# The routed experts' loop on TensorE, written out block by block, with its register loads moved

## The chip, the cores and the metric

The kernel runs on one core of one Trainium2 chip. The metric is the device time of one execution in microseconds (us). Three executions of the kernel before took 1186.09, 1189.49 and 1204.87 us; their median, 1189.49 us, is the time that the prediction is made against.

## The reference, cut to what matters

One transformer layer over x of shape (2, 2048, 512): a cross-attention by correlation against a context of 128 rows, and then a feed-forward part with a shared expert of 1024 hidden columns and 16 routed experts of 128 hidden columns. The change lies in the routed experts alone:

```python
topk_idx, w, _scores = _route(xf, router_w, correction_bias)   # 4 experts of 16 for each of 4096 rows
g = jnp.einsum('sc,ech->esh', xf, gate_w)                      # 512 -> 128
u = jnp.einsum('sc,ech->esh', xf, up_w)                        # 512 -> 128
h = jax.nn.silu(g) * u
hw = h * combine.T[:, :, None]                                 # the weights of the chosen four, else 0
routed = jnp.einsum('esh,ehc->sc', hw, down_w)                 # 128 -> 512
```

The kernel does not compute all 16 experts for all rows. It sorts the 4096 x 4 pairs of row and expert into blocks of 128 rows of one expert, and computes each block once.

## The kernel before, in words

Five programs, one for each engine, run side by side and meet in semaphores. The routed stage comes after attention, the shared expert of most rows and the routing. It handles `BLOCKS` = 144 blocks of 128 rows. Which expert a block belongs to is known only on the chip: VectorE writes a table `blocks_e`, and TensorE loads eight entries of it at a time into registers (`experts`, line 875) and uses them as addresses of the expert's weights, which lie in SBUF as high and low fp16 halves.

What happens to block s:

- GpSimd gathers its 128 rows from `xr_dram` into one of four buffers `xg` (an indirect DMA, line 1599, behind a small copy of indices, line 1587). Block s uses buffer s mod 4. For an odd block the buffer is free when the DMA that turned the rows of block s-4 has landed; for an even one, when TensorE has turned them. GpSimd issues the gathers strictly in order.
- The rows are turned so that the 512 input columns lie on partitions. Even blocks are turned by TensorE (`turn_rows`, 8 transposes, line 885) and copied out by VectorE (line 1463). Odd blocks are turned by a DMA transpose that SyncE issues (`turn_odd`, lines 538 and 539) into one of two buffers `xgT_odd`.
- `gate_up` (line 900): 12 matmuls, the gate and up columns together. ScalarE takes the silu (line 1116), VectorE multiplies (line 1477), ScalarE and VectorE split the product into high and low fp16 (lines 1120 and 1480).
- `turn_h` (line 911): two transposes of the product, copied out by VectorE (line 1469). `down` (line 919): three matmuls. ScalarE copies the result to SBUF (`save_y`, line 1126), one of two buffers, and SyncE writes it to `y_dram` (`y_out`, line 530).

TensorE's program is software-pipelined: in the step of block s it does `gate_up` of s+1, `turn_h` of s and `down` of s-1, with `turn_rows` of a later even block ahead of every second step. Four such steps are one pass of `four(i)`. The first pass is written out with constant counts; a loop (`pe.Fori`, line 940) makes the other 34 passes; the last steps are written out again. Inside the loop a semaphore count that depends on s is worked out in a register before the wait (lines 881, 892, 894, and parts of 883, 896 and 917), and each pass begins with `experts(4 * i)`, the register load of line 875.

SyncE's program is in order too. For each four blocks it issues: the turn of one odd block, two results out, the turn of the other odd block, two results out. A turn waits for its gather and for the `gate_up` that last read its buffer; a result waits for ScalarE's copy.

The other four engines keep their loops over the blocks.

Of the kernel before, what the change touches and what calls it, by code (L numbers as in the profile page):

```python
# [52 lines left out]
BLOCKS = (NP + E * (P - 1)) // P + 1  # L53
# [63 lines left out]
def build(nc, x, ctxT, wk, wqT, wv, wo, biases, bo, cb, routerT, gu_w, dn_w, const, const_r, out):  # L117
    with ExitStack() as ctx:
# [145 lines left out]
        def only(v, i, *rest):  # L264

            v = v[(slice(None), bass.ds(i, 1)) + rest]
            names = "abcd"[:len(v.shape) - 1]
            if len(v.shape) == 3:
                return v.rearrange("p a b -> p (a b)")
            return v.rearrange("p a b c -> p (a b) c")  # L270
# [330 lines left out]
        def _(pe):  # L601
# [181 lines left out]
            with pe.Fori(1, NB // 2) as i:  # L783

                a, b, s = 2 * i, 2 * i + 1, i - 1
# [87 lines left out]
            def experts(at):  # L873

                return nc.values_load_multi_w_load_instructions(
                    blocks_e[0:1, bass.ds(at, 8)], engines=[mybir.EngineType.PE], min_val=0, max_val=E - 1,
                    skip_runtime_bounds_check_because="VectorE counts at most E - 1 experts before a block")[1]

            def turn_rows(u, j, fresh):

                pe.wait_ge(s_xg[2 * j], 16 * ((u >> 1) + 1))
                if not fresh:
                    pe.wait_ge(s_txe, u - 1)
                for n in range(2 * KC):
                    last = turn(bank16[j][:, n * P:n * P + P], xg[:, 2 * j, n * P:n * P + P], id16)  # L885
                last.then_inc(s_tx, 1)

            def gate_up(s, r, e, fresh):

                j, rows = r % 2, (xgT, xgT_odd)[r % 2]  # L890
                if r % 2:
                    pe.wait_ge(s_odd[r // 2], 16 * ((s >> 2) + 1))
                else:
                    pe.wait_ge(s_txe, (s >> 1) + 1)
                if not fresh:
                    pe.wait_ge(s_rh, s - 1)
                n = 0
                for xv, wp in PARTS:
                    for kc in range(KC):
                        last = mm(bank[2 + j][:, 0:2 * H], rows[:, r // 2, xv * KC + kc, :],  # L900
                                  only((gu_hi_r, gu_lo_r)[wp], e, slice(kc * 2 * H, (kc + 1) * 2 * H)),
                                  start=(n == 0), stop=(n == 3 * KC - 1))
                        n += 1
                last.then_inc(s_rg, 1)

            def turn_h(s, j, fresh):
                pe.wait_ge(s_rhl, s + 1)
                if not fresh:
                    pe.wait_ge(s_hte, s - 1)
                for v in range(2):  # L910
                    last = turn(bank16[4 + j][:, v * P:v * P + P], r_hb[:, j, v, :], id16)
                last.then_inc(s_ht, 1)

            def down(s, j, e, fresh):
                pe.wait_ge(s_hte, s + 1)
                if not fresh:
                    pe.wait_ge(s_ye, s - 1)
                for n, (hv, wp) in enumerate(PARTS):
                    last = mm(bank[6 + j][:, :], r_hT[:, j, hv, :], only((dn_hi_r, dn_lo_r)[wp], e),  # L919
                              start=(n == 0), stop=(n == 2))  # L920
                last.then_inc(s_rd, 1)

            e = experts(0)
            turn_rows(0, 0, True)
            gate_up(0, 0, e[0], True)
            turn_rows(1, 1, True)
            gate_up(1, 1, e[1], True)
            turn_h(0, 0, True)
            def four(i, first):
                e = experts(4 * i)  # L930
                for n in range(4):
                    s = 4 * i + 1 + n
                    if n % 2:
                        turn_rows(2 * i + 2 + n // 2, n // 2, False)
                    gate_up(s + 1, (n + 2) % 4, e[n + 2], False)
                    turn_h(s, (1 + n) % 2, first and n == 0)
                    down(s - 1, n % 2, e[n], first and n < 2)

            four(0, True)
            with pe.Fori(1, BLOCKS // 4 - 1) as i:  # L940
                four(i, False)
            e = experts(BLOCKS - 4)
            gate_up(BLOCKS - 2, 2, e[2], False)
            turn_h(BLOCKS - 3, 1, False)
            down(BLOCKS - 4, 0, e[0], False)
            gate_up(BLOCKS - 1, 3, e[3], False)
            turn_h(BLOCKS - 2, 0, False)
            down(BLOCKS - 3, 1, e[1], False)
            turn_h(BLOCKS - 1, 1, False)
            down(BLOCKS - 2, 0, e[2], False)  # L950
            down(BLOCKS - 1, 1, e[3], False)


            pe.wait_ge(s_ye, BLOCKS)
# [733 lines left out]
```

## Time and profile before

| what | value |
|---|---|
| three executions | 1186.09, 1189.49, 1204.87 us |
| profiled execution: its span | 1205.0 us |
| profiled execution: its own time | not marked among the three; the longest, 1204.87 us, lies 0.13 us under the span |
| TensorE busy | 1046.4 us (87%) |
| VectorE, ScalarE, GpSimd busy | 638.2, 386.1, 444.0 us |
| DMA over the span | 191 GB/s on average |
| passes of the loop | from 571.4 to 944.4 us of the span |

Busy time is the union of an engine's instructions. TensorE's matmuls overlap, so its busy time counts a pipeline that is not empty, not one that is full. Instructions that an engine's sequencer handles alone (register operations, waits, branches, register loads, DMA issues) are not counted as busy; the profile marks them with a q behind the engine's name. "Issue" as a releaser means that the engine sat idle while nothing that the profile shows held it. The granted clock of TensorE is given as a share of 2.4 GHz.

### The profile page before, as it was taken

What the parts mean: (1) busy time and instruction counts of PE and PEld (TensorE: products, weight loads), DVE (VectorE), ACT (ScalarE), POOL (GpSimd) and SP (SyncE); (2) the same over time, 40 slices, a digit from 0 to 9 for tenths busy, and PEclk for the clock granted to TensorE, in tenths of its full rate; (3) what the DMA queues carried; (4) which work ended last, traced back from release to release, by engine and by line L of the source; (5) the groups of instructions that cost most, each with busy time, mean ns of one, the idle gap of its engine ahead of it and who ended that gap; (6) DMA issues with size and microseconds to landing.
All of it is one profiled execution on the core that took longest, in us unless ns stands there. A gap on an engine that the chain in (4) does not pass through costs nothing.

```text
span 1205.0 us, 22651 instructions
## 1 busy us (share of the span) xinstructions
PE 1046.4 (87%) x6496; PEld 603.5 (50%) x6497; DVE 638.2 (53%) x1454; ACT 386.1 (32%) x751; POOL 444.0 (37%) x517
## 2 busy tenths in 40 slices
PE   7899499899999988886789999889899877878597
PEld 6576344444444433434566676666666533323243
DVE  4935567533434877995333444434344246547455
ACT  2423243232323544441334443434344301111011
POOL 1730320111100424225334444344444286846650
PEclk9988789999999999997999999999999998989899
DMA  9605763563329315215999999989899686897750
GB/s 348 238 19 179 191 227 106 160 181 113 139 79 222 136 53 184 78 53 128 269 262 244 255 259 260 233 236 227 235 245 255 208 260 198 200 239 238 252 176 35
DMA packets 219262, 229.57 MB, mean 191 GB/s; under 512 B 143670, under 2 KB 152664, under 8 KB 218712
## 3 DMA queue, kind: packets, MB, share of 16 engines
q1 hardware_dynamic: 195676, 151.53, 44.1%
q0 software_dynamic: 23552, 77.61, 22.9%
q8 instruction: 17, 0.28, 0.1%
q14 instruction: 17, 0.14, 0.0%
HBM read 124.99 MB, written 70.55 MB: 162 GB/s over the span
## 4 chain that ended last, share of the span: by engine, by line
PE 44%; DVE 16%; issue 14%; DMA 13%; ACT 4%; another core or an unknown queue 4%; POOL 2%; SPq 1%; DVEq 1%; ACTq 0%; POOLq 0%
PE bank L750 13%; PE bank L900 11%; DMA arena<-arena 6%; PE bank L766 5%; PE bank L919 5%; DVE arena L1516 3%; DMA arena<-xr_dram,arena 2%; PE bank L731 2%; PE bank L885 2%; DVE arena L1274 2%; DVE arena L1450 1%; DMA y_dram<-arena 1%; DMA arena<-xr_dram 1%; PE bank L607 1%
## 5 line engine op out<-in xcount | busy, mean ns | idle before, releaser
L750 PE MATMUL bank<-arena 128*128 (+1 forms) x1536 | 361.3, 394 | 53.9 <-DVE arena L1274 27.3
L750 PEld LDWEIGHTS bank<-arena 128*128 128x128 f16 (+1 forms) x1536 | 154.1, 101 | 252.1 <-issue 65.2
L900 PE MATMUL bank<-arena 128*128 x1728 | 224.5, 278 | 34.0 <-issue 18.6
L900 PEld LDWEIGHTS bank<-arena 128*128 128x128 f16 x1728 | 162.8, 98 | 90.2 <-issue 55.9
L766 PE MATMUL bank<-arena 128*128 128x512 f16 (+1 forms) x768 | 176.2, 380 | 5.5 <-DVE arena L1276 5.5
L1599 POOL DMA_INDIRECT arena<-xr_dram,arena x144 | 141.2, 980 | 55.9 <-issue 43.9
L1629 POOL DMA_INDIRECT arena<-y_dram,arena x128 | 135.2, 1056 | 38.7 <-issue 34.2
L1477 DVE SCALAR_TENSOR_TENSOR arena<-bank,arena 128x128 f32<-128x128 f32 x144 | 41.9, 291 | 178.6 <-ACT arena L1116 140.4
L1053 ACT ACTIVATE arena<-arena 128x512 f16<-128x512 f32 x64 | 40.3, 630 | 262.1 <-DVE arena L1274 235.9
L766 PEld LDWEIGHTS bank<-arena 128*128 128x128 f16 x768 | 74.9, 98 | 96.9 <-DVE arena L1276 6.6
L919 PE MATMUL bank<-arena 128*128 x432 | 117.1, 380 | 0.7
L1274 DVE SCALAR_TENSOR_TENSOR arena<-bank,arena 128x512 f32<-128x512 f32 x64 | 44.0, 688 | 138.3 <-PE bank L750 82.0
L1516 DVE SCALAR_TENSOR_TENSOR arena<-arena 128x512 f32<-128x512 f32 x128 | 96.7, 759 | 29.7 <-DMA arena<-y_dram,arena 10.8
L1546 POOL TENSOR_TENSOR arena<-arena 128x2048 f16<-128x2048 f32 x8 | 32.5, 4066 | 200.8 <-ACT arena L1029 200.8
L1126 ACT ACTIVATE arena<-bank 128x512 f32<-128x512 f32 x144 | 84.5, 587 | 55.2 <-DMA y_dram<-arena 44.9
L1046 ACT ACTIVATE arena<-bank 128x512 f32<-128x512 f32 x64 | 38.0, 594 | 171.4 <-PE bank L750 132.3
L1587 POOL COPY arena<-arena 128x1 int32 (+1 forms) x144 | 26.8, 186 | 165.8 <-DMA arena<-arena 115.9
L1116 ACT ACTIVATE arena<-bank 128x128 f32<-128x128 f32 x144 | 39.8, 276 | 136.7 <-PE bank L900 103.5
L1572 POOL TENSOR_TENSOR arena<-arena 128x1024 f32 x16 | 34.2, 2137 | 128.2 <-ACT arena L1102 128.2
L1480 DVE TENSOR_TENSOR arena<-arena 128x128 f16<-128x128 f32 x144 | 42.2, 293 | 54.0 <-ACT arena L1120 45.4
L1276 DVE TENSOR_TENSOR arena<-arena 128x512 f16<-128x512 f32 x64 | 45.0, 702 | 46.2 <-ACT arena L1053 41.9
L1120 ACT ACTIVATE arena<-arena 128x128 f16<-128x128 f32 x144 | 44.5, 309 | 58.7 <-DVE arena L1477 47.4
(173 smaller groups left out, 1130.5 us busy)
## 6 DMA issues: line engine op xcount, KB each, us to landing
y_dram<-arena SPq DMA_DIRECT2D x144, 256.0 KB
arena<-in_x SPq DMA_DIRECT2D x8, 1024.0 KB, 12.4
xr_dram<-arena SPq DMA_DIRECT2D x16, 512.0 KB, 2.9
x_dram<-arena SPq DMA_DIRECT2D x8, 1024.0 KB, 4.7
arena<-x_dram SPq DMA_DIRECT2D x8, 1024.0 KB
arena<-in_gu_w SPq DMA_DIRECT2D x16, 512.0 KB, 3.2
x1s_dram<-arena SPq DMA_DIRECT2D x5, 1024.0 KB, 6.5
arena<-x1s_dram SPq DMA_DIRECT2D x20, 256.0 KB
```

The costliest lines, as they stand in the source:

```text
L750: last = mm(bank[g][:, :], w, xt(xv * KC + kc), start=(n == 0), stop=(n == 3 * KC - 1))
L766: last = mm(bank[2 + t][:, :], s_hb[:, half, hv, t * P:t * P + P], only((dn_hi_s, dn_lo_s)[wp], c), start=(first and n == 0), stop=(final ...
L900: last = mm(bank[2 + j][:, 0:2 * H], rows[:, r // 2, xv * KC + kc, :], only((gu_hi_r, gu_lo_r)[wp], e, slice(kc * 2 * H, (kc + 1) * 2 * H) ...
L919: last = mm(bank[6 + j][:, :], r_hT[:, j, hv, :], only((dn_hi_r, dn_lo_r)[wp], e), start=(n == 0), stop=(n == 2))
L1120: A(r_hb[:, j, 0, :], r_h[:, j, :], ACT.Copy).then_inc(s_rhh, 1)
L1126: A(y_sb[:, j, :], bank[6 + j][:, :], ACT.Copy, scale=1.0 / WS).then_inc(s_ye, 1)
L1274: V.scalar_tensor_tensor(s_h, bank[1][:, :], 1.0 / WS, s_silu, ALU.mult, ALU.mult).then_inc(s_sh32, 1)
L1276: V.tensor_tensor(s_hb[:, h, 1, :], s_h, s_hb[:, h, 0, :], ALU.subtract).then_inc(s_shl, 1)
L1480: V.tensor_tensor(r_hb[:, j, 1, :], r_h[:, j, :], r_hb[:, j, 0, :], ALU.subtract).then_inc(s_rhl, 1)
L1516: V.scalar_tensor_tensor(acc, ybuf[p % RING][:, e, :], w, acc, ALU.mult, ALU.add).then_inc(s_cmb, 1)
L1599: pool.indirect_dma_start(out=xg[:, r % 4, :], out_offset=None, in_=xr_dram[:, :], in_offset=bass.IndirectOffsetOnAxis(ap=token_now[:, r:r ...
L1629: pool.indirect_dma_start(out=ybuf[p % RING][:, e, :], out_offset=None, in_=y_dram[:, :], in_offset=bass.IndirectOffsetOnAxis(ap=row_now[: ...
```

## The change

TensorE's program of the routed stage no longer has a loop. All steps from block 1 to block 143 are written out with the same order of work inside a step, and every semaphore count is a constant. The registers of the next four blocks are loaded in the third step of each group of four (`ahead`), ahead of that step's `gate_up`, and are taken over (`here = ahead`) at the group's end; before, they were loaded at the head of the group that uses them. No matmul, no transfer and no other engine's program is changed.

```diff
-            e = experts(0)
+            here, ahead = experts(0), None
             turn_rows(0, 0, True)
-            gate_up(0, 0, e[0], True)
+            gate_up(0, 0, here[0], True)
             turn_rows(1, 1, True)
-            gate_up(1, 1, e[1], True)
+            gate_up(1, 1, here[1], True)
             turn_h(0, 0, True)
-            def four(i, first):
-                e = experts(4 * i)
-                for n in range(4):
-                    s = 4 * i + 1 + n
-                    if n % 2:
-                        turn_rows(2 * i + 2 + n // 2, n // 2, False)
-                    gate_up(s + 1, (n + 2) % 4, e[n + 2], False)
-                    turn_h(s, (1 + n) % 2, first and n == 0)
-                    down(s - 1, n % 2, e[n], first and n < 2)
-
-            four(0, True)
-            with pe.Fori(1, BLOCKS // 4 - 1) as i:
-                four(i, False)
-            e = experts(BLOCKS - 4)
-            gate_up(BLOCKS - 2, 2, e[2], False)
...
+            for s in range(1, BLOCKS):
+
+                n = (s - 1) % 4
+                if n == 2 and s + 2 < BLOCKS:
+                    ahead = experts(s + 1)
+                if n % 2 and (s + 3) // 2 < BLOCKS // 2:
+                    turn_rows((s + 3) // 2, n // 2, False)
+                if s + 1 < BLOCKS:
+                    gate_up(s + 1, (n + 2) % 4, here[n + 2], False)
+                turn_h(s, s % 2, s == 1)
+                down(s - 1, n % 2, here[n], s <= 2)
+                if n == 3:
+                    here = ahead
+            down(BLOCKS - 1, 1, here[3], False)
```

## Rows read from the trace of the kernel before

**Rows 1.** The page's first line: the span.

```profile
span 1205.0 us, 22651 instructions
```

**Rows 2.** Windows: length, busy (count) of PE, PEld, DVE, ACT, POOL, clock, DMA, GB/s.

```profile
613.60:746.60 133.00, 124.99 (x1091) 91.80 (x1089) 56.47 (x182) 57.13 (x156) 60.85 (x106) 1.00 0.97 255
746.60:944.40 197.80, 179.45 (x1517) 129.64 (x1515) 78.36 (x252) 79.97 (x217) 81.14 (x138) 0.98 0.92 237
571.40:613.60 42.20, 30.95 (x261) 21.86 (x260) 13.09 (x43) 13.85 (x37) 13.93 (x24) 1.00 1.04 266
```

**Rows 3.** Chain of waits, 613.6 to 746.6 us: shares of the stretch by line.

```profile
by line: PE bank L900 52.4%; PE bank L919 24.5%; PE bank L885 8.4%; issue 5.5%; PE bank L911 4.4%; another core or an unknown queue 2.4%; DVE arena L1477 0.7%; ACT arena L1116 0.6%; ACT arena L1120 0.6%; DVE arena L1480 0.5%; ACT arena L112
```

**Rows 4.** Chain of waits, 860 to 945 us, its pieces: start, length, what.

```profile
869.16 3.65 DMA arena<-xr_dram,arena
...
879.78 3.69 DMA arena<-xr_dram,arena
...
889.95 4.50 DMA arena<-xr_dram,arena
```

**Rows 5.** Timeline of TensorE's matmuls: start, length, line, count, idle time before.

```profile
810.33 1.47 PE L900 MATMUL bank<-arena 128*128 x12
...
812.85 1.47 PE L900 MATMUL bank<-arena 128*128 x12
...
815.83 1.63 PE L900 MATMUL bank<-arena 128*128 x12 [0.75 <-issue]
...
818.50 1.47 PE L900 MATMUL bank<-arena 128*128 x12
...
820.57 1.47 PE L900 MATMUL bank<-arena 128*128 x12
```

**Rows 6.** Waits of TensorE, 571.4 to 944.4 us: total us, times, longest.

```profile
PE bank L900 <- issue: 18.4, 28, 1.4
PE bank L900 <- DMA arena<-arena: 13.3, 13, 3.2
```

**Rows 7.** TensorE's sequencer by line: ns least/median/most, first and last start in us.

```profile
L875 PEldq TENSOR_LOAD <-arena x37: 588/703/1245, 553.0 to 944.4; - x37
L940 PEldq COMPARE_BRANCH  x34: 76/208/228, 584.6 to 944.3; - x34
L881 PEldq FUSED_REGOPS  x68: 82/88/96, 574.3 to 941.1; - x68
L894 PEldq FUSED_REGOPS  x68: 68/69/69, 572.4 to 938.8; - x68
```

**Rows 8.** Timeline of GpSimd: gathers of every second odd block.

```profile
612.47 0.98 POOL L1599 DMA_INDIRECT arena<-xr_dram,arena  x1 [0.50 <-POOL arena L1587]
...
622.39 0.98 POOL L1599 DMA_INDIRECT arena<-xr_dram,arena  x1 [0.50 <-PE bank L885]
...
632.66 0.98 POOL L1599 DMA_INDIRECT arena<-xr_dram,arena  x1 [0.50 <-POOL arena L1587]
```

**Rows 9.** Timeline of SyncE's issues: the turn of the first of these blocks.

```profile
616.36 1.51 SPq L539 DMA_TRANSPOSE arena<-arena  x1
```

**Rows 10.** Waits of SyncE's queue, 571 to 950 us: total us, times, longest.

```profile
SPq L530 <- ACT arena L1126: 113.0, 72, 4.4
SPq L538 <- DMA arena<-xr_dram,arena: 20.9, 22, 3.1
```

**Rows 11.** Waits of GpSimd, 571 to 950 us.

```profile
POOL arena L1587 <- DMA arena<-arena: 112.0, 48, 5.9
POOL arena L1587 <- PE bank L885: 41.2, 27, 4.5
```

**Rows 12.** DMA queues, 569.5 to 571 us: packets, MB, share of 16 engines.

```profile
q8 instruction: 1, 0.02, 4.0%
```

**Rows 13.** The same for 556 to 584 us.

```profile
q8 instruction: 2, 0.03, 0.4%
```

**Rows 14.** Timeline of TensorE's matmuls: the group that runs across the packet of rows 12.

```profile
570.44 1.47 PE L900 MATMUL bank<-arena 128*128 x12
```

More of the change, by code:

```diff
@@ L921, in down @@
                 last.then_inc(s_rd, 1)
-            e = experts(0)
+            here, ahead = experts(0), None
             turn_rows(0, 0, True)
-            gate_up(0, 0, e[0], True)
+            gate_up(0, 0, here[0], True)
             turn_rows(1, 1, True)
-            gate_up(1, 1, e[1], True)
+            gate_up(1, 1, here[1], True)
             turn_h(0, 0, True)
-            def four(i, first):
-                e = experts(4 * i)
-                for n in range(4):
-                    s = 4 * i + 1 + n
-                    if n % 2:
-                        turn_rows(2 * i + 2 + n // 2, n // 2, False)
-                    gate_up(s + 1, (n + 2) % 4, e[n + 2], False)
-                    turn_h(s, (1 + n) % 2, first and n == 0)
-                    down(s - 1, n % 2, e[n], first and n < 2)
-            four(0, True)
-            with pe.Fori(1, BLOCKS // 4 - 1) as i:
-                four(i, False)
-            e = experts(BLOCKS - 4)
-            gate_up(BLOCKS - 2, 2, e[2], False)
[L944 to L951, printed above, removed]
+            for s in range(1, BLOCKS):
[11 more added lines that the diff above has]
+            down(BLOCKS - 1, 1, here[3], False)
             pe.wait_ge(s_ye, BLOCKS)
```

## The prediction, made before the changed kernel ran

> **What bounds the kernel now.** I read the span first [rows 1], then the loop in windows. A pass of four blocks is 84 matmuls (48 of gate_up, 12 of down, 8 of turn_h, 16 of turn_rows), so the counts of [rows 2] say how many passes each stretch holds: 13 in 133.0 us (10.23 us a pass), 18 in 197.8 us (10.99), and 3 in the first 42.2 us (14.07). Three stretches, three regimes.
>
> In the middle stretch the chain of waits is TensorE's own: its four lines hold 52.4 + 24.5 + 8.4 + 4.4 = 89.7% [rows 3]. In the last stretch the chain often leaves TensorE: it goes from a gather through a DMA turn to the next gather into the same buffer, and the gathers in it start 10.62 and then 10.17 us apart [rows 4]. The first stretch is slow for TensorE's waiting on turned rows: of the loop's 13.3 us of such waits [rows 6], the longest is 3.2 us, and its DMA share is 1.04 [rows 2].
>
> Next the timeline of matmuls over one pass [rows 5]. A step without turn_rows starts 2.07 us after the one before it (818.50 to 820.57), one with turn_rows 2.52 us (810.33 to 812.85). Two of each are 9.18 us. At the loop's back edge the step takes 2.98 us instead of 2.07 (812.85 to 815.83, 0.75 us of it idle by "issue"), and the step after it 2.67 instead of 2.52, because the first group of twelve matmuls runs for 1.63 us instead of 1.47: it is fed as it is issued. Together 0.91 + 0.15 = 1.06 us, and 9.18 + 1.06 = 10.24 us is the middle stretch's pass of 10.23. So there TensorE is the bound, and the back edge is all it loses. Over 34 passes the idle time alone is 18.4 us [rows 6]; with what hides in matmul spacing it is at most 34 x 1.06 = 36 us.
>
> **The change part by part.** *Branch and loop counter.* 34 branches of 0.208 us [rows 7] leave the sequencer at the place where TensorE runs dry. *Counts.* Two register operations at line 881 of 0.088 us, two alike at line 892 and two at line 894 of 0.069 us leave each pass [rows 7], 0.49 us of sequencer time; the waits themselves stay. *Register load.* It is not removed: one for each four blocks, 0.588 to 1.245 us, median 0.703 [rows 7]. It moves from behind the branch to the head of the third step. As it is in the sequencer's order, what hides it is the work already handed to TensorE, and not the two blocks until its values are used. At the third step at least turn_h and down are queued behind gate_up: 2.07 - 1.47 = 0.60 us by [rows 5]. At the back edge the same queue left 18.4 / 34 = 0.54 us idle on average. Without the branch (0.21) and the head's threshold (0.07) that is 0.26 us; I take 0.25 us for the moved load, spacing included. Its bounds are nothing (hidden, as it should be with more lead) and 0.91 us (the gap just moves to the third step). The 0.49 us of sequencer work that goes speaks for the low end, the long loads for the high one. So TensorE's own pass becomes 10.24 - (1.06 - 0.25) = 9.43 us, between 9.18 and 10.09: alone worth 0.81 x 34 = 27 us, at most 36.
>
> The rows show the gap at the back edge 28 times [rows 6]. The Trainium skill, Advanced Engine Details and Errata, section Engine Queue Depths, gives TensorE a queue of 64 entries. By that, 32 matmuls with their weight loads would lie ahead, some 3.5 us by an estimate from the pass, and neither branch nor load could be felt: nothing to win, 1189 us. The trace does not agree: 0.75 us was idle behind them.
>
> *Code.* Straight code is fetched. Two packets came in the 28 us in which the written-out first pass ran [rows 13]; one packet held 4.0% of 16 engines over 1.5 us, that is one engine for 0.96 us [rows 12]. About one for each four steps is new, some 34. TensorE's group of twelve started and ran across that packet without an idle mark [rows 14]; I take nothing for TensorE, and nothing for the transfers, with 0.96 us a pass as the upper bound. DMA engines and other queues see no other new work.
>
> *What is late next.* The odd blocks' rows. The gather for block s+4 waits for the turn of block s, the turn of s+4 for that gather. Two rounds of this loop in the middle stretch took 9.92 and 10.27 us [rows 8], with 3.89 us from gather to turn and 6.03 us from turn to the next gather in the first of them [rows 8, 9]. GpSimd waited 112.0 us for turns, against 41.2 us for TensorE [rows 11]. So a second loop, without TensorE in it, runs at nearly TensorE's present pace, and 9.43 us is below all four rounds shown. It is not wholly free of TensorE: SyncE waited 113.0 us in 72 cases for results ahead of its turns and only 20.9 us in 22 for the gather itself [rows 10]; a faster TensorE takes some of that away.
>
> *The sum.* Middle stretch: a pass of 9.92 us, the shorter round, instead of 10.23: 0.31 x 13 = 4.0 us. Bounds: 0 (10.27 holds) and 0.81 x 13. Last stretch: 0.2 x 18 = 3.6 us, between 0 (the chain of [rows 4]) and 0.81 x 18; I take near the low end because four tenths of its 10.99 us and more are above both loops and are not the back edge. First stretch: 0, it waits for data. Together 8 us; the end after the loop moves with it. The profiled span of 1205.0 becomes 1197 us. It is 15.5 us longer than the median of the runs, 1189.5, which the change should move by as much: **1181.5 us**.
>
> **The rivals.** *A. TensorE's gain passes through.* For it: the chain of [rows 3], and SyncE's 113.0 us, which make turns late for TensorE's sake, so that the row loop would shrink along. Against: [rows 8] and [rows 4], rounds without TensorE that take 9.92 to 10.62 us. 27 us: 1162 us; with no cost of the load left, 1153 us.
>
> *B. Nothing moves.* The load stops the sequencer as long in the third step (the 0.91 us end), or the row loop holds 10.2 us everywhere; the change then doesn't do what its text says. For it: the load is still in order, and the gather rounds average 10.25 us over [rows 4, 8], equal to the pass. Against: the branch and counts do go. 1189 us.
>
> *C. Slower: fetched code on the row loop.* Each pass brings a packet that holds one DMA engine for 0.96 us [rows 12]; a turn or gather has landed only when its last engine is done, so a packet in the wrong place lengthens a round by as much. In every pass: 34 x 0.96 = 33 us, less the 8: 1214 us. It decides the sign from 0.24 us a pass, which eats the 8 us, and 2% from 0.94 us. For it: a DMA share of 0.92 to 1.04 [rows 2]. Against: [rows 14], and that half the rounds have slack by [rows 10]. The Trainium skill, DMA: Bandwidth & Descriptors, section Queues, rings and completion order, has each engine alternate between queues and finish a whole packet first. By that rule such a packet does delay its engine's other work; no run here yet shows by how much a turn was late for it.
>
> **How the numbers follow.** Forecast 0.57, A 0.20, B 0.15, C 0.08. The range takes in A's 1162 and B's 1189, with room for the spread of the runs seen: 1160 to 1194 us. Outside lie C, A's extreme and noise, under 2 in 10. Around 2% is what a measurement of this kernel can tell from no change: below 1165.7 us or above 1213.3 us. Faster by that: most of A, 0.14, and 0.02 of the forecast's tail, so 0.16. Slower: most of C, 0.06. Within: 0.78.
>
> **What would show it.** No branch on TensorE; its waits by "issue" at gate_up down from 18.4 us to under 9; waits for turned rows (13.3 us) and for gathers on SyncE (20.9 us) up, since the bound moves there; passes of 9.9 to 10.1 us in a calm stretch. Passes of 9.4 us with TensorE's lines in the chain mean A. The same "issue" time, in the third step, means B. About 34 packets on q8 must appear; idle time on TensorE just behind them, or turns that land later by about 1 us, mean C. The forecast is wrong if the row loop's round falls well below 9.9 us.

## The result, and the profile after

The changed kernel took 1217.37 us (median of 4 executions, 1209.3 to 1221.29), the kernel before on the same occasion 1190.07 us (4 executions): ratio **1.019 [1.014, 1.024]**. It is slower; the prediction was 1181.5 us, in a range that ended at 1194. Run again later beside other kernels, it took 1225.91 us against 1209.21 us, 1.012 [1.004, 1.019]. The medians here take in every execution, and each ratio, with its interval, only those in the faster of the two states in which executions come, so that it is not the quotient of the medians.

A measure for these ratios: the kernel before, measured twice against itself, came out at 1.009 [1.003, 1.016] and at 0.995 [0.989, 1.001]. So the intervals are too narrow by about a hundredth, and a difference of about one per cent or less is called none. The loss itself is 16.7 to 27.3 us by the medians.

The page of the changed kernel, its span and its DMA queues (packets, MB, share of 16 engines), stands against [rows 1]:

```profile
span 1214.8 us, 22342 instructions
...
q1 hardware_dynamic: 195676, 151.53, 47.0%
q0 software_dynamic: 23552, 77.61, 22.7%
q8 instruction: 45, 0.74, 0.3%
```

q1 carries the turns of odd blocks and the results, q0 the gathers, q8 fetched code. Before, q8 had 17 packets and q1 needed 44.1% of a span of 1205.0 us for the same 195,676 packets. That is 16 x (0.470 x 1214.8 - 0.441 x 1205.0) = 633 us more of engine time for the same bytes; q0 has no more than before (22.9%).

The windows of the changed kernel, with the columns of [rows 2]:

```profile
571.40:613.60 42.20, 32.08 (x249) 22.72 (x248) 12.77 (x41) 13.12 (x36) 12.86 (x22) 0.84 1.03 231
613.60:746.60 133.00, 119.78 (x1000) 85.64 (x998) 51.86 (x167) 51.91 (x143) 56.35 (x96) 0.97 1.00 239
746.60:944.40 197.80, 174.61 (x1465) 125.25 (x1464) 75.73 (x243) 78.00 (x210) 82.11 (x140) 0.98 1.01 233
```

At 84 matmuls a pass the middle stretch now takes 11.2 us a pass (10.23 before), the last one 11.3 (10.99). In these two stretches the DMA share rose while GB/s fell. The chain of waits of the middle stretch answers to [rows 3], where TensorE's four lines held 89.7%:

```profile
by line: DMA arena<-arena 40.8%; PE bank L900 24.5%; DMA arena<-xr_dram,arena 11.4%; PE bank L919 10.8%; issue 5.0%; PE bank L885 3.0%; PE bank L911 2.0%; another core or an unknown queue 1.5%; ACT arena L1117 1.4%; DVE arena L1468 1.1%; AC
```

Turns and gathers hold 52.2%, TensorE 40.3%. The two profiles compared here lie further apart than the kernels do. The chain of the same stretch in the third profile of the kernel before, and in the second of the changed kernel:

```profile
by line: PE bank L900 34.1%; DMA arena<-arena 29.6%; PE bank L919 14.6%; DMA arena<-xr_dram,arena 9.6%; issue 5.2%; PE bank L885 4.7%; PE bank L911 2.8%; ACT arena L1126 1.3%; DVE arena L1477 1.1%; ACT arena L1116 1.1%; SPq L530 0.9%; ACT a
```

```profile
by line: PE bank L900 22.7%; DMA arena<-arena 18.4%; DMA y_dram<-arena 10.9%; PE bank L919 10.7%; issue 9.7%; DMA arena<-xr_dram,arena 8.1%; PE bank L885 3.0%; SPq L539 3.0%; ACT arena L1117 2.3%; SPq L530 2.0%; PE bank L911 1.9%; another c
```

TensorE holds 56.2% in the one (78.4% in the kernel's second profile) and 38.3% in the other. By the counts of matmuls a pass of this stretch takes 10.8 us in the second and third profiles of the kernel before, and 11.2 us in both of the changed kernel; the last stretch takes 10.7 to 11.0 us in the former and 10.9 and 11.3 in the latter.

TensorE's waits (571.4 to 944.4 us), SyncE's and GpSimd's (571 to 950 us), and its register load (least/median/most ns) follow; they answer to [rows 6, 10, 11, 7].

```profile
PE bank L900 <- DMA arena<-arena: 30.4, 20, 7.6
...
PE bank L900 <- issue: 2.2, 8, 0.6
```

```profile
SPq L538 <- DMA arena<-xr_dram,arena: 28.0, 28, 3.2
```

```profile
POOL arena L1578 <- DMA arena<-arena: 150.3, 54, 9.9
...
POOL arena L1578 <- PE bank L885: 21.9, 18, 3.0
```

```profile
L875 PEldq TENSOR_LOAD <-arena x36: 587/690/1914, 553.1 to 961.5; - x36
```

The gap by "issue" did go, from 18.4 to 2.2 us (14.7 and 14.8 in the other profiles of the kernel before, 4.7 in the second of the changed one), and GpSimd waits for turns 38.3 us longer (112.0 to 150.3; the other profiles have 118.4 and 126.2 before, 139.1 after). TensorE waits for turned rows instead in this pair of profiles (13.3 to 30.4 us), but that does not separate the kernels: it is 19.8 and 22.6 us in the other two before, and 19.4 in the second after.

**The row loop, measured.** A round of an odd block is: gather from issue to its last packet, time until SyncE issues the turn, turn from issue to its last packet, time until the next gather into the same buffer is issued. The table gives means in us over the 46 to 56 rounds, from the seventh four blocks on, whose packets can be told apart (64 of 4,096 bytes a gather, 1,024 of 256 bytes a turn), and the mean time of one turn packet over the routed stage. Its kernels are those of the experiments below.

| kernel | gather | to the turn | turn | to the next | round | turn packet, ns |
|---|---|---|---|---|---|---|
| before | 4.03 | 1.43 | 3.58 | 1.67 | 10.71 | 25.0 |
| before, second profile | 3.95 | 1.28 | 3.76 | 1.69 | 10.67 | 26.1 |
| before, third profile | 4.00 | 1.10 | 3.85 | 1.73 | 10.69 | 27.7 |
| changed | 4.25 | 0.97 | 4.17 | 1.76 | 11.14 | 33.4 |
| changed, second profile | 4.10 | 1.14 | 4.16 | 1.62 | 11.01 | 30.4 |
| written | 4.25 | 0.93 | 4.01 | 1.78 | 10.97 | 32.3 |
| inject4 | 4.24 | 1.18 | 4.14 | 1.97 | 11.53 | 33.1 |
| deep | 3.94 | 2.76 | 3.75 | -0.10 | 10.35 | 21.9 |
| deep4 | 4.03 | 2.64 | 3.84 | -0.25 | 10.26 | 23.5 |
| deep_after | 4.76 | 2.95 | 4.21 | -1.36 | 10.56 | 30.9 |

From before to changed (means over their profiles) the turn takes 0.44 us more and the gather 0.18, and the time to the turn shrinks by 0.22: 0.39 us a round, 13 us over 34 passes, of a loss of 17 to 27 us. In the profiled executions that is about all of it: their spans average 1205.3 us before and 1215.9 changed, and the gate_up of block 24 begins 78.1, 85.6 and 86.4 us after the first gather before, 85.8 and 80.7 us changed, so the loss lies behind it. Where the rest of the 17 to 27 us goes, no trace shows. A round is as long as a pass whatever holds the pass, so its length alone does not say that this loop is the bound; `deep`, below, tests that.

### The profile page after: what moved, and what is told of

It reads as the page before. It is cut to its first block, busy times and chain, and to the rows that moved or that the text cites. A ratio compares the mean times of both kernels' runs of the same rounds, so it can differ in the third digit from the quotient of the medians.

```text
span 1214.8 us, 22342 instructions
## 1 busy us (share of the span) xinstructions
PE 1055.9 (87%) x6496; PEld 606.7 (50%) x6496; DVE 638.8 (53%) x1454; ACT 387.0 (32%) x751; POOL 447.9 (37%) x517
## 3 DMA queue, kind: packets, MB, share of 16 engines
q1 hardware_dynamic: 195676, 151.53, 47.0%
## 4 chain that ended last, share of the span: by engine, by line
PE 36%; DMA 21%; DVE 15%; issue 13%; another core or an unknown queue 5%; ACT 4%; POOL 3%; SPq 1%; DVEq 1%; POOLq 0%; ACTq 0%
PE bank L750 14%; DMA arena<-arena 11%; DMA arena<-xr_dram,arena 6%; PE bank L766 6%; PE bank L900 5%; PE bank L919 2%; DMA y_dram<-arena 2%; POOL arena L1620 2%; DVE arena L1507 2%; PE bank L731 2%; DVE arena L1441 1%; DVE arena L1265 1%; PE bank L607 1%; PE bank L627 1%
## 5 line engine op out<-in xcount | busy, mean ns | idle before, releaser
L750 PE MATMUL bank<-arena 128*128 (+1 forms) x1536 | 356.8, 390 | 38.3 <-ACT arena L1037 14.2
L900 PE MATMUL bank<-arena 128*128 x1728 | 228.7, 282 | 39.1 <-DMA arena<-arena 32.9
L900 PEld LDWEIGHTS bank<-arena 128*128 128x128 f16 x1728 | 165.9, 100 | 96.8 <-issue 60.7
L766 PE MATMUL bank<-arena 128*128 128x512 f16 (+1 forms) x768 | 179.0, 382 | 10.7 <-DVE arena L1267 8.8
L766 PEld LDWEIGHTS bank<-arena 128*128 128x128 f16 x768 | 75.1, 99 | 103.7 <-DVE arena L1267 10.5
L919 PE MATMUL bank<-arena 128*128 x432 | 120.5, 389 | 0.6 <-DVE arena L1460 0.3
L1265 DVE SCALAR_TENSOR_TENSOR arena<-bank,arena 128x512 f32<-128x512 f32 x64 | 44.1, 689 | 133.5 <-PE bank L750 76.4
```

Source lines behind the costliest of these rows:

```text
L750: last = mm(bank[g][:, :], w, xt(xv * KC + kc), start=(n == 0), stop=(n == 3 * KC - 1))
L766: last = mm(bank[2 + t][:, :], s_hb[:, half, hv, t * P:t * P + P], only((dn_hi_s, dn_lo_s)[wp], c), start=(first and n == 0), stop=(final ...
L1265: V.scalar_tensor_tensor(s_h, bank[1][:, :], 1.0 / WS, s_silu, ALU.mult, ALU.mult).then_inc(s_sh32, 1)
```

## The experiments

**Pace or fetched code.** The change does two things at once: it feeds TensorE better, and it makes it fetch code all the time. `paced` takes the first back: eight useless matmuls of 256 columns, some 0.87 us, ahead of the first gate_up of each four blocks of the changed kernel.

```diff
+                for _ in range(extra):
+                    mm(bank[2 + j][:, 0:2 * H], rows[:, r // 2, 0, :], gu_hi_r[:, 0, 0:2 * H], start=True, stop=True)
```

> The changed kernel, written out, with eight matmuls of no use ahead of the first gate_up of each four blocks (0.109 us each, 0.87 us a pass, overwritten by the true ones), so that TensorE's own pass is as long as before, about 10.2 us, while the code is fetched as in the changed kernel and a little more. Theory F: 1210 to 1230 us, turn packets at 33 ns or more. Theory P: back to 1190 us, turn packets near 25 ns.

1221.45 against 1202.41 us, 1.013 [1.003, 1.023]; 48 packets on q8, 32.7 ns a turn packet. With TensorE held up by 0.88 us a pass (808.75 to 809.63 us in its trace) turn packets are still longer on average, and the ratio lies above one still, if little above what the kernel before showed against itself.

`written` is the other half: the kernel before with its loop written out, the register load left at the head of each four blocks.

```diff
-            with pe.Fori(1, BLOCKS // 4 - 1) as i:
+            for i in range(1, BLOCKS // 4 - 1):
                 four(i, False)
```

> The loop of before written out and nothing else: the register load stays at the head of each four blocks, without lead. Theory F (the instruction packets stretch the DMA turns, and the row loop with them): some 30 packets on q8 in the routed stage, a turn's packet of 256 bytes from 25 ns to 31-34 ns, ratio 1.010 to 1.020. Theory P (the loss comes from a TensorE that runs ahead, the fetch costs nothing): TensorE's gap at each four blocks is still there, so the ratio is 0.995 to 1.005.

1219.26 against 1208.47 us, 1.014 [0.999, 1.028]; on time alone that is no clear difference. The trace is clear. DMA queues from 613.6 to 930 us, first of the kernel before, then of written, then of the changed kernel:

```profile
q1 hardware_dynamic: 78544, 46.22, 57.1%
```

```profile
q1 hardware_dynamic: 77397, 45.21, 63.7%
...
q8 instruction: 25, 0.41, 0.6%
```

```profile
q1 hardware_dynamic: 76368, 44.74, 65.1%
...
q8 instruction: 25, 0.41, 0.6%
```

Twenty-five packets of code, 0.6% of the engines' time, go with 6.6 to 8.0 points more for q1, which moves less than before in that stretch. With the other profiles (58.2 and 60.2% before, 61.6% changed) the step is smaller and has the same sign. Per MB, q1's share is 1.24 points in the kernel before (57.1 / 46.22; 1.25 and 1.29 in its other profiles), 1.41 in written and 1.46 in the changed kernel. Of all kernels here, those without steady fetching lie at 1.13 to 1.31 and those with it at 1.35 to 1.46; inject4, below, lies at 1.42. The waits of TensorE in written, 571 to 950 us:

```profile
PE bank L900 <- DMA arena<-arena: 32.6, 21, 7.9
...
PE bank L900 <- issue: 3.5, 11, 0.8
```

The gap by "issue" is nearly gone here too, without any lead for the load.

**Which turns are longer.** Not all of them, and not all packets: the median turn packet takes 18 ns in both kernels, and the mean rises by a few long ones. Of the 61,440 packets of the 60 turns from the seventh four blocks on, 49, 73 and 97 took over 1 us in the profiles of the kernel before, 436 and 335 in those of the changed kernel, and 380 in written. In the changed kernel some nine in ten of these begin within 3 us of the start of a packet of code. The turns can be parted by whether a packet of code was on an engine while they ran:

| kernel | turns with code | us | packets over 1 us in each | turns without | us | packets over 1 us in each |
|---|---|---|---|---|---|---|
| before, three profiles | 0 | | | 60 | 3.64 to 3.81 | 0.8 to 1.6 |
| changed | 27 | 4.60 | 14.5 | 33 | 3.93 | 1.3 |
| changed, second profile | 22 | 4.67 | 13.1 | 38 | 3.72 | 1.2 |
| paced | 30 | 4.70 | 8.8 | 30 | 3.22 | 0.5 |
| written | 24 | 4.09 | 12.2 | 36 | 3.93 | 2.4 |

A turn that meets a packet of code has about ten times the long packets and takes 0.67 and 0.95 us more in the changed kernel (0.16 in written, whose other turns hold some more long packets too); the others are much as before. A longer turn meets a packet more easily, but chance moments laid on the turns of the kernel before pick turns at most 0.2 us longer than its mean. Packets of results (2,048 bytes) and of gathers (4,096) did not get longer on average: 88.9 and 245.8 ns before, 87.5 and 241.7 changed (613.6 to 930 us).

**TensorE's pace without fetching.** Here the loop stays, with 1, 4, 8 or 17 passes a body, and the load moves to the head of the third step:

```diff
+            def group(p, final=False):
+                e = experts(4 * p + 2)
+                for m in range(4):
+                    n, s = (m + 2) % 4, 4 * p + 3 + m
...
+            with pe.Fori(0, 8) as i:
+                for w in range(4):
+                    group(4 * i + 2 + w)
```

> One part of the change alone: the loop of one pass a body stays, with its 34 branches and counts in registers; only the register load stands ahead of the third step and not of the first. No code is fetched in the loop. Theory F and theory P both expect about the kernel before, 1185 to 1195 us, since branch and load still stand together; under P it could lose a little if TensorE gets faster by it.

> TensorE keeps a loop, but of 8 iterations of four passes each (16 blocks a body); two passes and the ends are written out, and the registers are loaded ahead of the third step, as in the changed kernel. So TensorE is nearly as fast as in the changed kernel (26 of 34 branches gone), while its code should be fetched once and then stay. Theory F (the 16 KB packets of fetched code hold up the DMA turns of the odd blocks): few packets on q8 in the loop, turn packets back near 25 ns on average, total at or under the kernel before, 1175 to 1190 us. Theory P (a faster TensorE alone makes turns, gathers and result writes collide; the fetches are innocent): turn packets stay near 33 ns and the total stays at 1205 to 1220 us.

> The same program as the loop of four passes a body, but with 17 passes a body and 2 iterations: a body too long to stay, as far as one can guess, so that about 28 packets of code come over q8 in the routed stage, at the same pace of TensorE. Theory F: 1205 to 1220 us, like the changed kernel. Theory P: the same time as the loop of four passes a body. If few packets come on q8, it says nothing against F and should be as fast as the short body.

All three were far slower, and for a reason that had nothing to do with the question: 1.090 [1.081, 1.100], 1.080 [1.070, 1.090] and 1.083 [1.074, 1.093]. Register load and waits of TensorE (571 to 1040 us) in loop1:

```profile
L875 PEldq TENSOR_LOAD <-arena x37: 777/2573/5071, 551.2 to 1041.5; - x37
```

```profile
PE bank L900 <- issue: 93.7, 34, 4.8
```

The load's median went from 703 ns [rows 7] to 2,573. It now starts at entry 4p + 2 of the table, 8 bytes off a multiple of 16. The next kernels move the table by two entries, so that the same load starts at such a multiple:

```diff
-        blocks_e = little(BLOCKS + 8, I32)
+        blocks_e = little(BLOCKS + 12, I32)[:, 2:BLOCKS + 10]
```

> The loop of four passes a body again, with the table of experts moved by two entries, so that each register load starts at a multiple of four entries (16 bytes) as in the kernels before and after; in the first trial the load started two entries off and took 2.8 us. If the start is what made it slow, loads are back at 0.6 to 1.2 us and the total falls by about 100 us. Theory F (fetched code holds up the turns): few packets on q8 in the loop, turn packets near 25 ns, total 1165 to 1190 us on a chip where the kernel before takes 1190, so a ratio of 0.98 to 1.00. Theory P (a faster TensorE alone makes the transfers collide): ratio 1.01 to 1.02, turn packets at 33 ns.

> The same program with 8 passes a body and 4 iterations. If the code of eight passes stays, it is as fast as the loop of four passes or 1 to 3 us faster, with few packets on q8; if it is fetched anew in each iteration, theory F puts it with the loop of 17 passes and theory P with the loop of four.

> The same program with 17 passes a body, and the table moved likewise. The first trial showed 48 packets on q8, 30 of them in the routed stage, as many as in the changed kernel. Theory F: slower than the loop of four passes by 1.5 to 3%, ratio to the kernel before 1.01 to 1.02, turn packets at 30 ns or more. Theory P: the same as the loop of four passes.

> The loop of before with one pass of four blocks a body, the load moved to the head of the third step and its address at a multiple of 16 bytes; nothing is written out but the first and last blocks. Theory F: no fetch in the loop, turn packets at 25 ns, the load's lead no longer needed by anything: ratio 0.995 to 1.005. Theory P: ratio 1.005 to 1.015, as with four passes a body. If the load still takes 2.8 us the misaligned address was not the cause, and the ratio is near 1.09.

even4 took 1213.87 us, 1.010 [1.005, 1.015]; even1 1210.1 us, 1.011 [1.005, 1.017]; both are called none, if barely: on its own occasion even1 stands beside a kernel before that came out at 1.009. even8 took 1230.6 us, 1.026 [1.022, 1.030]; even17 1225.27 us, 1.017 [1.012, 1.023]. The median load is 0.73 to 0.88 us again in all four. The queues of even4 and of even8, 613.6 to 930 us:

```profile
q1 hardware_dynamic: 78769, 46.09, 60.4%
...
q8 instruction: 3, 0.05, 0.1%
```

```profile
q8 instruction: 30, 0.49, 0.7%
```

A body of four passes is fetched once and then runs without fetching; a body of eight is fetched again in each round. The two kernels with the fetching are the slower ones: turns that meet a packet of code take 4.25 us in even8 and 4.44 in even17, the others 3.66 and 3.58. But their time does not show what that costs, because a second cost came with it: TensorE itself waits for code where the loop jumps back. The branch and TensorE's waits by "issue" (571 to 950 us) in even8, then the branch in even4:

```profile
L951 PEldq COMPARE_BRANCH  x4: 79/4958/5689, 698.4 to 978.8; - x4
```

```profile
PE bank L900 <- issue: 26.1, 16, 6.5
```

```profile
L951 PEldq COMPARE_BRANCH  x8: 76/208/231, 645.0 to 950.5; - x8
```

The three jumps back of even8 leave TensorE idle for 6.4, 6.5 and 4.8 us, 17.6 us in all, about as much as the 16.7 us by which it is slower than even4; the one of even17 leaves 4.4 of 11.4 us. The written-out kernels have no jump and no such wait. The two loops without steady fetching did not win either: waits by "issue" were 8.0 us in even4 and 21.2 in even1, and neither number shows in the time. So by time alone kernels with and without fetching are hardly parted (paced 1.013, written 1.014; even4 1.010, even1 1.011); it is the turns that part them.

**Packets of that size by themselves.** ScalarE issues copies of 16,372 bytes from DRAM to DRAM, outside the computation, in the kernel before: one a pass (inject) or one a block (inject4).

```diff
+                for n in range(4):
+                    act.dma_start(spare_dram[bass.ds(4 * i + n, 1)], gu_flat).then_inc(s_spare, 16)
```

> The kernel before, and for each pass of its loops ScalarE issues one copy of 16372 bytes in HBM whose result nothing reads (35 of them), sized so that it should not be cut over the DMA engines. This puts the suspected traffic alone into the kernel before. Theory F: turn packets above 28 ns, and the total up by 8 to 30 us (ratio 1.007 to 1.025), if the copy goes as one long packet on one engine; if the trace shows it in short packets over many engines it tells less. Theory P: ratio 1.00, turn packets at 25 ns.

> The kernel before with one copy of 16,372 bytes from DRAM to DRAM for each block, four a pass, issued by ScalarE; the copies are not part of the computation. Theory F: four times the disturbance of one copy a pass (1.004, 27.3 ns): turn packets 31 to 36 ns, ratio 1.012 to 1.022. Theory P: DMA traffic of this size is hidden, ratio 0.998 to 1.006.

inject: 1205.6 against 1198.73 us, 1.004 [1.000, 1.009], a turn packet 27.3 ns, within what three profiles of the kernel before show. inject4: 1244.83 against 1208.47 us, 1.046 [1.036, 1.056], a turn packet 33.1 ns. A turn that met one of inject's copies had 4.1 packets over 1 us, against 13 to 15 in a turn of the changed kernel that met code; it took 4.69 us, but the other turn of the pass was shorter, and the mean is 3.88. So large packets do stretch turns, but it took 140 of them to do what some 30 packets of code do, and inject4 is not a clean dose: each issue holds ScalarE's queue for 0.587 us (median), 2.3 us a pass, and its round is 0.4 us longer than the changed kernel's at equal turns. Why packets of code weigh so much more is not shown.

**Latency or throughput of the row loop.** `before_again`, `before_third` and `after_again` are the two kernels once more.

> The kernel before, unchanged, for a second profile of it: ratio 0.997 to 1.003; shows how far one profile's stages differ from another's. Both theories expect turn packets of 25 ns and 17 packets on q8; the wait of TensorE by issue at gate_up 15 to 20 us.

> The kernel before, unchanged, as a control: 0.997 to 1.009, which is what no change measures.

> The changed kernel again, beside the others of this call. If its loss is real it stands 1 to 2% above the kernel before and above before_third; if it was the spread of that measurement, within 0.7% of both.

Their ratios stand above. `deep` gives each odd block a second buffer for its gathered rows, in 4 KB a partition that is free in this stage, so that a gather waits for the turn of the block eight before. `deep_after` is the changed kernel with the same buffers.

```diff
+        xg_new = view(o1 + 4 * KB, [2, 2 * D], F16)
+        odd_rows = [[xg[:, 1, :], xg_new[:, 0, :]], [xg[:, 3, :], xg_new[:, 1, :]]]
...
-                        pool.wait_ge(s_odd[r % 4 // 2], 16 * (s >> 2))
+                        behind = (s - 4) >> 2
+                        if not isinstance(s, int) or behind:
+                            pool.wait_ge(s_odd[r % 4 // 2], 16 * behind)
```

> The kernel before with two buffers for the gathered rows of each odd block, so that a gather waits for the turn of the block eight before and not four before. Theory L (the row loop is held by its latency): GpSimd's waits for turns (112 us) fall below 40 us, the late stretch comes down from 10.99 to TensorE's 10.24 us a pass, ratio 0.980 to 0.992. Theory D (DMA throughput is the bound): GpSimd's waits fall, but turns and gathers then take longer by as much, SyncE's waits for gathers do not vanish, ratio 0.995 to 1.009.

> The changed kernel with the same two more buffers. Theory L: now nothing but TensorE holds a pass, and the gap that the change removed turns into time: a pass of 9.4 to 9.9 us, ratio 0.965 to 0.985. Theory D: the instruction packets still stretch the turns (33 ns a packet), TensorE's waits for turned rows stay at 30 us or more, ratio 1.005 to 1.02.

deep: 1188.75 against 1209.21 us, 0.980 [0.974, 0.986]. deep_after: 1196.43 us, 0.989 [0.984, 0.994], short of the 0.965 to 0.985 expected. The latency of the loop was what held the stage: deep moves the same bytes in turns as long as before (3.75 us), and GpSimd has no wait for a turn left. (SyncE's loop holds eight blocks in deep instead of four; that was not tried by itself.) Windows (columns of [rows 2]), the chain from 626 to 930 us, and the waits of TensorE and of GpSimd (571 to 950 us) in deep:

```profile
613.60:746.60 133.00, 122.47 (x1086) 91.72 (x1084) 56.23 (x182) 56.71 (x155) 60.73 (x104) 1.00 0.94 253
746.60:930.00 183.40, 168.08 (x1496) 126.15 (x1492) 77.30 (x250) 78.43 (x213) 79.51 (x135) 1.00 0.93 251
```

```profile
by line: PE bank L905 52.8%; PE bank L924 24.8%; PE bank L890 8.5%; issue 7.6%; PE bank L916 4.3%; another core or an unknown queue 1.5%; DVE arena L1482 0.2%; ACT arena L1121 0.2%; ACT arena L1125 0.2%; DVE arena L1485 0.1%; ACT arena L113
```

```profile
PE bank L905 <- issue: 25.7, 31, 1.2
PE bank L905 <- DMA arena<-arena: 6.5, 3, 3.3
```

```profile
POOL arena L1592 <- PE bank L890: 152.0, 65, 6.8
```

Gate_up is line 905 here, the turn on TensorE line 890. Both stretches run at 10.3 us a pass (10.3 and 10.4 in its second profile), TensorE's four lines hold 90.4% of the chain, and the gap by "issue" is back at 25.7 us. In deep_after, 626 to 930 us and 571 to 950 us, the turns are still in the chain and in TensorE's waits:

```profile
by line: PE bank L905 34.7%; DMA arena<-arena 21.3%; PE bank L924 14.6%; issue 8.2%; DMA y_dram<-arena 6.2%; PE bank L890 4.3%; ACT arena L1122 2.8%; PE bank L916 2.3%; SPq L533 1.6%; DVE arena L1473 1.1%; ACT arena L1116 0.9%; ACT arena L1
```

```profile
PE bank L905 <- DMA arena<-arena: 18.7, 15, 5.0
PE bank L905 <- issue: 11.5, 18, 1.7
```

**Is TensorE's gap worth anything?** `deep4` has the buffers of deep and the loop of even4: no fetching, load moved, branch in every fourth pass only. `deep_again` stands beside it.

> deep with TensorE's loop of four passes a body, the register load two blocks ahead and at a multiple of 16 bytes (the loop of even4). Theory L (row loop by latency, gap on TensorE behind it, fetch on the turns): no fetch in the loop and the gap gone, so a pass of 9.5 to 10.0 us instead of deep's 10.32, ratio 0.962 to 0.978, below deep by 8 to 25 us. Rival Q (something else, such as ScalarE's y copies or SyncE's order, holds 10.3 us): same as deep, 0.977 to 0.987.

> deep unchanged, for comparison on the same chip: 0.974 to 0.987, waits by issue at gate_up about 26 us.

deep4: 1189.52 against 1209.84 us, 0.987 [0.978, 0.997]; deep_again 1196.41 us, 0.995 [0.990, 1.000]. The two differ by 0.6% in the medians, which is no difference by the control. TensorE's waits (571 to 950 us), its register load and a pass of its timeline in deep4:

```profile
PE bank L905 <- issue: 24.7, 30, 1.5
PE bank L905 <- DMA arena<-arena: 9.3, 4, 3.4
```

```profile
L880 PEldq TENSOR_LOAD <-arena x37: 592/909/2120, 552.8 to 936.4; - x37
```

```profile
760.20 1.63 PE L905 MATMUL bank<-arena 128*128 x12 [1.32 <-issue]
...
762.88 1.47 PE L905 MATMUL bank<-arena 128*128 x12
...
764.95 1.47 PE L905 MATMUL bank<-arena 128*128 x12
...
767.46 1.47 PE L905 MATMUL bank<-arena 128*128 x12
...
770.71 1.49 PE L905 MATMUL bank<-arena 128*128 x11 [1.01 <-issue]
```

The gap did not go; it sits ahead of the third step's gate_up, where the load now is. From 620 to 915 us the load takes 0.90 us on average and TensorE idles 0.80 us behind it, with 2.8 matmuls still to finish when it begins; in deep it was 0.93, 0.82 and 3.2. In the changed kernel it was 0.83, 0.17 and 7.1: more work was queued there when the load began, it seems because TensorE had just waited for data.

deep and deep4 are the kernels that beat both: by the medians of their runs 1.1 to 1.7% under the kernel before. Repeated, the gain of deep was 0.5 to 2.0%.

## Why the prediction was wrong

**What bounds the kernel.** The row loop stood in the prediction as what is late next, at 9.9 to 10.6 us. It was already the bound in many passes: a pass averages 10.69 us over three profiles, and with the loop's latency out of the way the stage runs at 10.3 us. That TensorE alone held the middle stretch [rows 3] was true of the one profile that was read; in the kernel's other two a pass takes 10.8 us there, and TensorE holds 78.4 and 56.2% of the chain.

**Branch and counts: right, and worth nothing.** They went, and in deep4, which drops three branches of four, no time followed.

**Register load: the first step that failed.** The sum took 0.25 us for the moved load and so 9.43 us for TensorE's pass. Measured, where TensorE is the bound, the load costs 0.80 us of idle time wherever it stands, near the bound of 0.91, and a pass in deep4 is 133.0 / (1096 / 84) = 10.2 us. The gap of [rows 5] was the load's nearly alone, not the branch's. Rival B had this mechanism; the time did not stay, because of the next step. The "issue" time of the changed kernel (2.2 us) came as forecast but, by the matmuls still queued at the load, for another reason: waits for rows cover it. So that sign, read alone, would have confirmed a step that failed.

**Code: the step that decided.** "I take nothing for TensorE, and nothing for the transfers": the first half held, the second did not. A turn takes 0.44 us more and a gather 0.18, under the bound of 0.96 us a pass that rival C paid in full. C named the place and the form, one packet in the way of one turn, and its 1214 us lies near the result. In the changed kernel 27 and 22 of 60 turns met a packet of code and took 0.67 and 0.95 us longer than the others, up to C's 0.96; not every packet cost a round that much, as C had it. What C did not have is how a turn is stretched: it came to hold 13 to 15 packets over 1 us, where one engine held the code. From 611 to 946 us the time of turn packets above 18 ns each sums to 997 and 808 us of the engines in the changed kernel (459 to 594 before); 367 and 255 us of it lie under a packet of code on any engine, and 691 and 601 us in the half of the packets that begin within 3 us of the start of one. The Trainium skill, Runtime: NRT & Kernel Launch, section Instruction fetch mechanics, calls crossing a 16 KiB boundary "mostly hidden". For TensorE's own issue in straight code the traces agree ([rows 14], 2.2 us by "issue"); for the turns that run beside the code they do not (4.60 us, 3.93 without).

**What is late next.** SyncE's waits for gathers rose as forecast (20.9 to 28.0 us; 14.1 and 12.2 in the other profiles before, 22.9 in the second after). TensorE's for turned rows rose in the first pair of profiles only. The time that a faster TensorE can take out of the round, 1.27 us on average before, fell to 1.06: SyncE's slack was real, and smaller than what the turns and gathers lost.

**The sum.** Minus 8 us became plus 17 to 27. The gain was nothing: where the row loop held the passes TensorE's pace did not count, and where TensorE held them (deep, deep4) the moved load cost what the gap had cost. The cost was the term set to zero: the longer turns and gathers account for 13 us, worked out from the rounds; time alone does not show that share. The 0.08 for C was too little: the DMA share of 0.92 to 1.04 [rows 2], with the turn in the chain of [rows 4], was a reason to price the bound of 0.96 us there rather than drop it.

**What is open.** How one packet of code comes to stretch a dozen packets of a turn, and why it does so more than a copy of the same size; whether the 0.9% between deep and deep_after is theirs, as its chain suggests, since deep_again and deep_after cannot be told apart by time.

## What to carry to other kernels

Before a loop is written out, look at which DMA work lies on the critical path: steady code fetching is small in bytes and can still lengthen transfers made of many small packets. One profile of each kernel is not enough to read a shift of waits from: here two profiles of the same kernel differed in TensorE's share of a chain by over 30 points. A wait that disappears from an engine shows that its cover has changed, not that its cost has gone; check it in a variant where that engine is the bound. Where a chain goes through a buffer's release, a second buffer is worth trying before a faster engine is.

## What the runs showed of the hardware

- A load of eight table entries into TensorE's registers took 0.59 us at best and 0.60 to 0.93 us at the median where it starts at a multiple of 16 bytes (single ones up to 3.2 us), and 1.9 to 5.3 us (median 2.5 to 2.6) in loop1, loop4 and loop17, where it starts 8 bytes off a multiple of 16. The Trainium skill, DMA: Bandwidth & Descriptors, section Latency and other measured facts, gives a register load a floor of about 600 ns; the best loads agree, and it does not speak of the start address.
- While such a load runs, TensorE lives on what was handed to it: 2.8 to 7.1 matmuls were left to finish when it began in deep4, deep and the changed kernel, with 0.80 to 0.17 us of idle time behind it.
- A loop body of four passes needed 8 packets of code in the whole routed stage, one of eight passes 38. The jump back to the head of the longer body took 4.3 to 5.7 us, that of the shorter one 0.21.
- The turns that ran beside a packet of code, in the changed kernel, held 13 to 15 packets over 1 us, the others 1.2 to 1.3; packets of results and gathers did not get longer on average.
- One profile of the same kernel can differ from another by 8 us in its first passes: the gate_up of block 20 began 68.2 us after the first gather in the profile that the prediction read, and 75.5 and 76.4 us after it in the two later ones.
